# Value products of two cross attentions in eight one-round blocks instead of four two-round ones, small copies moved to ScalarE, later weights moved down the queue

## The reference, cut to what matters

```
q = x @ q_w + q_b ; k = ctx @ k_w + k_b ; v = ctx @ v_w + v_b       # split into 16 heads of 16
scores = einsum('bhqd,bhkd->bhqk', q, k) / 4 ; masked where mask_BxS2 is set
x = x + einsum('bhqk,bhkd->bhqd', softmax(scores), v)
```

## Time and the profile before

| what | value |
|---|---|
| median of 3 runs | 2120.66 us (2118.71 to 2126.54) |
| the profiled execution | 2128.31 us, span 2127.0 us, mean granted clock 0.959 |
| steps of the two cross attentions | from about 62 to 516 us, and from about 741 to 1180 us of the span |
| PE busy over the span | 1913.0 us (90%) |
| DVE, ACT, POOL busy | 1384.7, 1145.9, 490.6 us |

### The profile page before, as it was taken

How to read it: one execution, slowest core, us unless ns; L and a number is a source line. 1 busy time by engine, 2 the same in 40 slices (tenths; PEclk the granted TensorE clock), 3 DMA queues, 4 the chain that set the end, 5 groups by cost and what they waited for, 6 DMA issues and landing times.

```text
span 2127.0 us, 36546 instructions
## 1 busy us (share of the span) xinstructions
PE 1913.0 (90%) x13543; PEld 1203.1 (57%) x13543; DVE 1384.7 (65%) x3339; ACT 1145.9 (54%) x2619; POOL 490.6 (23%) x663
## 2 busy tenths in 40 slices
PE   7999999987998899999999789998899799898998
PEld 4555655544474455565555455547646588564656
DVE  3787668875667578667888465541246998477473
ACT  3676677765354277667777451142145687174252
POOL 2111011111640211101100150000024366264251
PEclk9999999999999799999999889999899899999999
DMA  9677667770111857667762202252100432200110
GB/s 204 148 142 131 114 119 159 133 154 1 40 29 45 135 111 143 129 117 155 148 90 32 82 4 90 78 174 80 65 20 8 133 110 80 85 1 8 40 53 11
DMA packets 114223, 191.45 MB, mean 90 GB/s; under 512 B 17096, under 2 KB 67072, under 8 KB 107520
## 3 DMA queue, kind: packets, MB, share of 16 engines
q1 hardware_dynamic: 113056, 188.11, 40.2%
q10 hardware_dynamic: 992, 1.02, 0.2%
HBM read 135.20 MB, written 2.69 MB: 65 GB/s over the span
## 4 chain that ended last, share of the span: by engine, by line
PE 68%; DVE 18%; ACT 8%; issue 3%; DMA 2%; SPq 1%; POOL 1%; DVEq 0%; ACTq 0%; POOLq 0%
PE PS L786 9%; PE PS L677 8%; PE PS L346 8%; DVE WK L849 6%; PE PS L694 5%; PE PS L354 4%; PE PS L706 4%; PE PS L664 4%; ACT WK L960 3%; PE PS L1807 3%; PE PS L1832 3%; PE PS L455 3%; PE PS L2182 2%; PE PS L2240 2%; PE PS L482 2%
## 5 line engine op out<-in xcount | busy, mean ns | idle before, releaser
L849 DVE TENSOR_REDUCE WK<-PS 128x1 f32<-128x1024 f32 x512 | 609.0, 1220 | 223.0 <-PE PS L677 162.6
L960 ACT ACTIVATE WK<-PS 128x512 f32<-128x512 f32 x840 | 445.4, 605 | 103.4 <-PE PS L677 102.0
L677 PE MATMUL PS<-QSR,KSR 51*128 51x256 f32 x2048 | 392.2, 310 | 61.1 <-DVE QSR L862 24.6
L677 PEld LDWEIGHTS PS<-QSR,KSR 51*128 51x128 f32 x2048 | 265.1, 187 | 251.5 <-ACT WK L960 102.7
L664 PE MATMUL PS<-KSR,QSR 51*128 51x512 f32 x1024 | 390.5, 465 | 10.7 <-DMA KSR<-scratch_mask 4.0
L664 PEld LDWEIGHTS PS<-KSR,QSR 51*128 51x128 f32 x1024 | 186.1, 188 | 22.8 <-issue 14.7
L786 PE MATMUL PS<-WK 128*32 128x256 f32 x2528 | 191.8, 388 | 0.0
L554 ACT ACTIVATE WK<-PS,WK 128x256 f32<-128x256 f32 (+1 forms) x320 | 140.3, 451 | 78.9 <-DVE WK L522 49.6
L1036 POOL TENSOR_SCALAR nbw<-WK 128x4 fp32r<-128x4 f32 x64 | 12.6, 197 | 603.2 <-PE PS L677 285.6
L580 POOL TENSOR_TENSOR WK<-WK 128x128 f32<-128x128 f32 (+1 forms) x128 | 64.8, 506 | 341.2 <-DVE WK L540 306.1
L983 POOL TENSOR_TENSOR WK<-WK 128x512 fp32r<-128x512 f32 x62 | 79.1, 1277 | 232.0 <-ACT WK L928 121.9
(11 more groups left out here) (340 smaller groups left out, 3374.4 us busy)
## 6 DMA issues: line engine op xcount, KB each, us to landing
KSR<-WK SPq DMA_DIRECT2D x381, 128.0 KB
WB<-in_ctxT SPq DMA_DIRECT2D x78, 512.0 KB, 5.2
WK<-in_ctxT SPq DMA_DIRECT2D x40, 512.0 KB, 4.0
WA<-in_ctxT SPq DMA_DIRECT2D x26, 512.0 KB, 5.1
WK<-in_ctx SPq DMA_DIRECT2D x8, 1024.0 KB, 5.3
WK<-in_ctx SPq DMA_DIRECT2D x16, 512.0 KB, 4.4
QSR<-scratch_q SPq DMA_DIRECT2D x48, 128.0 KB, 4.1
WB<-in_L3f_qkv SPq DMA_DIRECT2D x2, 1536.0 KB, 6.4
```

Source lines behind the costliest of these rows:

```text
L677: return pe.e.matmul(tile["S", L, s, i][:, j * 256:j * 256 + 256], KS[s % 4][HALF[i % 2], kt * 128:(kt + 1) * 128], QS[HALF[i % 2], g % 2, ...
L849: dv.e.tensor_reduce(mt[:, n:n + 1], tile["R", L, s, n].rearrange("p a b -> p (a b)"), AX, ALU.max).then_inc(*dv.at("R", L, s, n))
L960: ac.e.activation(PR[n % NPR], tile["S", L, s, i], ACT.Exp).then_inc(*ac.at("E", L, s, i))
```

## The change

Seven edits:

1. PE's score tiles are listed one at a time instead of two; the order of the matmuls inside a pair stays.
2. F goes from four blocks of two rounds, behind tiles 3, 7, 11 and 15, to eight blocks of one round, one behind every odd tile. Its first block of a step moves from behind tile 7 to behind tile 5.
3. K moves from behind the pair of tiles 8 and 9 to between the two, and V from behind tiles 4 and 5 to between them.
4. M moves from behind tile 15 to behind tile 13 and its F block.
5. The copy of L862 moves from DVE to ACT, as does E0. ACT takes its two QSR copies ("MC") between the exponentials of tiles 12 and 13.
6. ACT's E0 stands behind the exponential of tile 3, and the next step's F waits for ACT.
7. In L = 0 the self attention's weights are issued at step 28 (`last`) instead of at step 24, thus behind all ST.

```diff
-        for i in range(0, 16, 2):
+        for i in range(16):
             n = 4 + i // 2 if i < 8 else i // 2 - 4
             r = s + (1 if i < 8 else 2)
-            row = (r, n) if r < 32 else None
-            yield "U", s, i, row
+            yield "U", s, i, (r, n) if r < 32 else None
             yield "S", s, i
-            if row:
+            if i % 2 and r < 32:
                 yield "R", r, n
-            yield "S", s, i + 1
-            if i == 2 and s:
-                if s + 1 < 24:
-                    yield "L", s + 1
-                yield "F", s - 1, 3
+            if i == 2 and 0 < s < 23:
+                yield "L", s + 1
+            if i == 1 and s:
+                yield "F", s - 1, 24, 28
+            if i == 3 and s:
+                yield "F", s - 1, 28, 32
+            if i == 5:
+                yield "F", s, 0, 4
...
+            if i == 15:
+                yield "F", s, 20, 24
+            if i == 3 and s:
                 yield "E0", s - 1
+            if i == 8 and s < 24:
+                yield "K", s // 4 + 2, s % 4
             if i == 4 and 8 <= s < 16:
                 yield "V", 1, s - 8, s
-            if i in (6, 10, 14):
-                yield "F", s, i // 4 - 1
-            if i == 8 and s < 24:
-                yield "K", s // 4 + 2, s % 4
-            if i == 14:
+            if i == 12:
+                yield "MC", s + 1
+            if i == 13:
                 yield "M", s + 1
...
-                    for u in range(2):
-                        column_bank(s, i + u)
-                        if row and u == 0:
-                            row_bank(*row)
-                        column(s, i + u, 0)
-                        if row and u == 0:
-                            row_half(*row, 1)
-                        elif row:
-                            row_half(*row, 0).then_inc(*pe.at("R", L, *row))
-                        column(s, i + u, 1).then_inc(*pe.at("S", L, s, i + u))
+                    column_bank(s, i)
+                    if row and i % 2 == 0:
+                        row_bank(*row)
+                    column(s, i, 0)
+                    if row and i % 2 == 0:
+                        row_half(*row, 1)
+                    elif row:
+                        row_half(*row, 0).then_inc(*pe.at("R", L, *row))
+                    column(s, i, 1).then_inc(*pe.at("S", L, s, i))
...
-                elif o[0] == "E0":
-                    s = o[1]
-                    dv.wait_ge(pe, "F", L, s, 7)
...
-                    dv.e.tensor_copy(PVS, bank[7].ap[:, 0:256]).then_inc(*dv.at("E0", L, s))
...
-                elif o[0] == "M" and o[1] < 32:
+                elif o[0] == "E0":
+                    s = o[1]
+                    ac.wait_ge(pe, "F", L, s, 7)
+                    if s:
+                        ac.wait_ge(pe, "E1", L, s - 1, 1)
+                    ac.e.activation(PVS, bank[7].ap[:, 0:256], ACT.Copy).then_inc(*ac.at("E0", L, s))
+                elif o[0] == "MC" and o[1] < 32:
                     s = o[1]
                     g, hh, bb, h = where(s)
                     ac.wait_ge(pe, "M", L, s, 1)
+                    ac.e.activation(QS[32:34, g % 2, hh, :], tile["M", L, s][32:34, 0, 0:256], ACT.Copy).then_inc(*ac.at())
...
+                elif o == ("S", 28, 0) and L == 0:
+                    last()
```

More of the change, by code:

```diff
@@ L129, in xattn_first @@
         yield "ST", 3
-        between = {1: (("K", 1, 1),), 4: (("K", 1, 2), ("L", 0)), 7: (("K", 1, 3), ("L", 1)), 10: (("M", 0),)}
+        between = {1: (("K", 1, 1),), 4: (("K", 1, 2), ("L", 0)), 7: (("K", 1, 3), ("L", 1)), 10: (("M", 0), ("MC", 0))}
         for n, r in enumerate([*rowmax(0), *rowmax(1)][:12]):
@@ L169, in xattn_order @@
     for s in range(32):
[L170 removed]
+        for i in range(16):
             n = 4 + i // 2 if i < 8 else i // 2 - 4
             r = s + (1 if i < 8 else 2)
[L173 to L174 removed]
+            yield "U", s, i, (r, n) if r < 32 else None
             yield "S", s, i
[L176 removed]
+            if i % 2 and r < 32:
                 yield "R", r, n
[L178 to L182 removed]
+            if i == 2 and 0 < s < 23:
[6 more added lines that the diff above has]
+                yield "F", s, 0, 4
+            if i == 7:
+                yield "F", s, 4, 8
+            if i == 9:
+                yield "F", s, 8, 12
+            if i == 11:
+                yield "F", s, 12, 16
+            if i == 13:
+                yield "F", s, 16, 20
+            if i == 15:
+                yield "F", s, 20, 24
+            if i == 3 and s:
                 yield "E0", s - 1
+            if i == 8 and s < 24:
+                yield "K", s // 4 + 2, s % 4
             if i == 4 and 8 <= s < 16:
                 yield "V", 1, s - 8, s
[L186 to L190 removed]
+            if i == 12:
+                yield "MC", s + 1
+            if i == 13:
                 yield "M", s + 1
@@ L193, in xattn_order @@
             yield "ST", s + 4
-    yield "F", 31, 3
+    yield "F", 31, 24, 28
+    yield "F", 31, 28, 32
     yield "E0", 31
@@ L760, in xattn_pe @@
                     if s >= 2:
-                        pe.wait_ge(dv, "E0", L, s - 2)
+                        pe.wait_ge(ac, "E0", L, s - 2)
                         for q in range(2):
@@ L770, in xattn_pe @@
                 elif o[0] == "F":
-                    _, s, c = o
+                    _, s, m0, m1 = o
                     g, hh, bb, h = where(s)
-                    if c == 0:
+                    if m0 == 0:
                         if s:
-                            pe.wait_ge(dv, "E0", L, s - 1)
+                            pe.wait_ge(ac, "E0", L, s - 1)
                         else:
@@ L778, in xattn_pe @@
                                 pe.wait_ge(*event)
-                        pv.owner = ((dv, "E0", L, 31),)
+                        pv.owner = ((ac, "E0", L, 31),)
                         pe.wait_ge(ac, "V", L, bb, 7)
-                    for m in range(8 * c, 8 * c + 8):
+                    for m in range(m0, m1):
                         i, j = m // 2, m % 2
@@ L858, in xattn_dve @@
                     s = o[1]
[L859 to L862, removed]
                     if s >= 2:
@@ L1091, in stack, with xattn_sp @@
                 sp.e.dma_start(KSW[s % 4][64 * u + 34:64 * u + 35, :], scr[L:L + 1, a:a + 2048]).then_inc(*d_ks[s % 4].at(L, s))
-        def xattn_sp(L, later, constants=None):
+        def xattn_sp(L, later, last=None, constants=None):
             if L:
@@ L1232, in later, with last @@
                 sp.e.dma_start(cv, tiles(D["L0f_cv"])).then_inc(*d_l0f.at())
+            def last():
                 for n, kt, m, at in L0A:
@@ L1236, in later @@
                 sp.e.dma_start(sm[:, 6:8], D["L0a_b"]).then_inc(*d_l0a.at())
-            xattn_sp(0, later, constants)
+            xattn_sp(0, later, last, constants)
         L0A, a0 = [], 0
```

5 lines of the change are left out of this document (1 added, 4 removed).

## The result

| | before | after |
|---|---|---|
| median of four runs each | 2119.68 us (2118.16 to 2126.54) | 2188.93 us (2186.47 to 2190.16) |
| the profiled execution | 2128.31 us | 2186.47 us, span 2185.1, mean granted clock 0.964 |
| PE busy | 1913.0 us | 1936.1 us (89%) |
| DVE, ACT, POOL busy | 1384.7, 1145.9, 490.6 us | 1347.5, 1203.2, 490.4 us |

The ratio after to before is 1.0319, with a 95% interval of 1.0294 to 1.0343: the kernel became slower by about 69 us. The forecast was 2167 with a range of 2130 to 2195: the time lies inside the range, but the loss is half again the 46.6 us that were forecast.

The account below looks back on a forecast made before the run. PE sets step lengths, with small idle waits. Per layer, K steps +14.4, K+V steps +20.1, plain -5.1, last -3 make 26.4 us; twice, less 6.2, is +46.6 on 2120.7: 2167, 8-in-10 range 2130 to 2195.

Parts of the forecast that it names:

- The new unit (G = 1.24): On PE, a pair of score tiles plus one F round takes 1.24 us, winning 0.14 per four tiles.
- Rival B: Turns between F and score tiles on PE cost a full drain: +45 us, 2212 us; chance 5%.
- K between tiles 8 and 9: K waits 0.38 us for its banks, tile 10 waits 0.82 for DVE's reduce; K step 14.05 against 13.15, +0.90.
- V between tiles 4 and 5: The same waits around V, which takes 3.65 us; step with K and V 19.02 against 16.51, +2.51.
- M behind tile 13: Near a step's end, M costs 0.57 us and its ring turn adds a wait of 0.24; old QSR wait gone.
- The plain step: Steps without K and V: 10.80 us against 11.53, -0.73 each.
- The wait at a step's start: PE's wait for QSR copies, 29 times and 11.7 us in layer 0's steps before, would be gone.
- E0 on ACT: Queued behind exponential 3, E0 makes the next step's F wait about 0.07 us; hidden where V stands.
- rival C: ACT becomes the bound: E0 0.5 us later than timed loses 31 us over 62 steps, 2198 us; chance 4%.
- The weights: Issuing the self attention's weights behind all ST removes step 26's 6.25 us excess over a plain step: -6.2 us.
- Steps without row tiles: The last one and a half steps of each layer: at most 3.3 us gained per layer, 3 taken.
- Rival A: The split of row tiles by K and V costs nothing: faster by 30 us, 2090 us; chance 10%.

Follow-up runs that it names:

- Experiment 2: Changed kernel with K behind its whole pair and F round, V still splitting tiles 4 and 5: 2138.74 us, one run, beside 2126.58 for the kernel before.
- experiment 7: Changed kernel with ACT's two QSR copies queued behind the exponential of tile 13, not of tile 12: 2191.76 us, one run, beside 2129.93 for the kernel before.
- experiment 4: Changed kernel with E0 and the copy of two QSR rows back on DVE: 2207.75 us, one run, beside 2123.43 for the kernel before.
- Experiment 5: Changed kernel with the two absolute-sum passes over feed-forward weights moved from step 25 to step 26: 2179.29 us, one run, beside 2123.43 for the kernel before.
- experiment 6: Changed kernel with the self attention's weights issued at step 24 again: 2186.91 us, one run, beside 2126.58 for the kernel before.
- experiment 3: Kernel before with only K put between tiles 8 and 9 and V between tiles 4 and 5: 2278.51 us, one run, beside 2123.43 unedited.
- experiment 1: Changed kernel with K and V behind whole pairs and their F round: 2124.03 us, 10 runs, beside 2123.43 for the kernel before, ratio 1.0005.

## Why the prediction was right, point by point

The mechanism was the forecast's; its size was short by a third, and one term of the sum failed, that of the weights. Counted in the two profiled executions, the two cross attentions (first M to last value product) became 31.3 and 35.0 us longer, and the rest of the program 8 shorter: 58.2 between these executions, where 46.6 were forecast. The medians are 69 apart, because the profiled execution of before is 8.6 above its median and that of after 2.5 below.

- **The new unit (G = 1.24): right.** Pairs are 1.24 apart (386.44 to 387.68). Rival B, with 1.4 or more, is out, and with it the full drain of the Trainium skill's "TensorEngine Tiling (Array Packing)" (Key Properties) as a visible cost: the turns cost what the earlier trace rows show, about 0.1 each way, and no run shows one alone.
- **K between tiles 8 and 9: right in all its parts.** K began 0.82 behind tile 8 (forecast 0.81), tile 9 at 2.69 (2.67), tile 10 at 4.59 (4.49). The 0.1 is the price of a release: DVE's end to PE's start is 0.14 to 0.15 where I had estimated 0.05. The two waits of PE are 0.32 and 0.84, 1.16 together (forecast 1.20). The step is 14.22 for 14.05.
- **V between tiles 4 and 5: right,** 19.19 for 19.02, by the same term. Experiment 2 adds that the length of V doesn't matter.
- **M behind tile 13: right, with the same term.** From M to the next tile 0.90 was measured where 0.57 + 0.24 were forecast. The program and DVE's rows (under experiment 7) say that it is the ring and not the copies; no experiment shows it, since the copies did not move in that one. The plain step came out at 10.86 for 10.80. The wait at a step's start, 11.7 us in 29 places, is gone as forecast; what carries the copies' name now, 7.7 us in layer 0, is by the same reading the ring's.
- **E0 on ACT: right.** F waits 0.2 us at most in layer 1, so rival C is out. In step 25 it waits 6.5 us, but with E0 on DVE that step is as long (experiment 4).
- **The weights: the term of the sum that was wrong.** I counted -6.2 for edit 7. Step 26 did come down from 17.78 to 10.87 and its wait for KSR went, but step 25 went from 14.35 to 19.79. The two together fell by 1.5 us, no more than two plain steps' own gain of 1.3. The failed step is that I took the place where PE waited, step 26, as the only one that a load could hold, and did not look at step 25, where ACT has passes queued that wait for the feed-forward part's loads. These were in time by 0.3 us before and now come 4.4 us late, and all that stands behind the pass waits, E0 and exponentials alike. Experiment 5 shows the mechanism (step 25 back at 10.92), experiment 4 that E0's move is worth 0.4 us of it at most, and experiment 6 that without edit 7 PE would wait for KSR only 1.1 us.
- **Steps without row tiles:** 3 us per layer were forecast. The last whole step is 10.37, only 0.5 below the other plain ones, and from the last M to the last value product nothing was gained (12.49 before, 12.58 after). The term was 2.6 us per layer too hopeful.

Summed per layer: K steps 16 x 1.07 = 17.1 (14.4 forecast), K+V steps 8 x 2.68 = 21.4 (20.1), plain ones 7 x -0.67 = -4.7 (-5.1), the last ones -0.4 (-3): 33.4 against 26.4. Layer 1 shows 35.0, as its first step went from 16.22 to 17.70; layer 0 31.3, as its first step stayed (20.07 to 19.95) and some of its K steps had been longer before (13.70 once, 13.57 once). The 8 us won elsewhere were not forecast, and 4.1 of them, ahead of the first step, are scatter and no effect of the change: the first step begins at 62.45 before and at 58.33 after, but at 58.18 in experiment 3, where the work ahead of it is that of the kernel before, and at 61.26 and 61.16 in experiments 6 and 7, where it is that of the changed one. For the other 4 no cause is known.

Rival A had the right question and the wrong answer. Without the splits the kernel is at 2124, not at 2090. Of these 34 us some 14 are steps with K and V that are longer than A had them (13.19 and 13.01 for 12.85, 17.10 and 16.93 for 16.62), 7 are steps 25 and 26 and 5 the last steps; of the rest, 3 us are the chip of experiment 1, on which the kernel before took 2123.43 and not the 2120.7 that A starts from, and 5 were not traced.

## What to carry to other kernels

Don't put long work between two instructions that together fill one buffer. The reader can't begin beforehand, so its time comes on top instead of beside, and in a ring of two the next user but one pays for it: here 1.0 to 1.2 us a place whether the work put in took 1.9 or 3.7. When an operation moves in a ring, ask of each of its neighbours who had the same buffer two turns ago and when that was read.

Look at each step that differs from the steady one, and ask of each load that an engine waits for in its queue by how much it was in time. Here it was 0.3 us, and with shorter steps and a slower load it came 4.4 us late. Then everything behind the wait stands still: with the small copy there PE sat idle for 6.5 us, with the copy on another engine for 4.1 behind an exponential, and the step was as long.

A releaser in a profile can be a mere neighbour in time. Look up in the program what the waiting instruction asks for. If you move the named instruction to test it, check in the rows that it has moved: in experiment 7 it stood later in the list and ran at the same moment.

## What was not expected of the hardware

The granted clock, in experiment 3. A K step of about 15 us has one idle place of 1.40 us on PE there, beside three of 0.2 to 0.4, and in 24 of the 46 steps with K, the first of each layer left out, the clock fell from 2.4 to 1.2 GHz for a part of the step (mean 0.80, 17.30 us for 14.92). In the changed kernel, whose idle places in a K step are 0.84, 0.32 and 0.26 us, it stayed at 1.00 in every such step but layer 1's first. So such a stall cost up to 2.4 us more than itself. The Trainium skill ("TensorE: Matmul & The Clock Gate", Part 1) has the default state as throttled, and activity as what releases it. These runs agree in the direction: it fell where PE was idle for more of the step.

A release from DVE to PE takes 0.146 us (DVE's end to PE's start, 386.295 to 386.441), three times my estimate. A load of 16 KB needed 10.5 us from issue to landing, behind two of 1 MB each in the same queue, and 8.2 in the kernel before.
